# A two-layer block on one core: the broadcast inverse root mean squares written by ScalarE instead of copied by VectorE

## The reference, cut to what matters

```
proj = hidden_states @ W_in.T
u, gate = jnp.split(proj, 2, axis=-1)
... (causal convolution over 4 taps, silu)
ssm_p = u @ Wx.T
dt, Bm, Cm = jnp.split(ssm_p, [R, R + N], axis=-1)      # 32, 16 and 16 columns
dt = _rmsnorm(dt, dt_ln_w)      # x * rsqrt(mean(x * x) + 1e-6) * w
Bm = _rmsnorm(Bm, b_ln_w)
Cm = _rmsnorm(Cm, c_ln_w)
delta = jax.nn.softplus(dt @ Wdt.T + dt_bias)
# state = exp(delta * A) * state + delta * u * B;  y = sum(state * C), over 2048 tokens
```

## Time and profile before

| | |
|---|---|
| median of 3 runs | 2167.95 us (2166.07 to 2169.68) |
| the profiled execution | 2169.23 us |
| its span, first to last instruction | 2167.4 us |
| TensorE, granted clock | 0.804 of full |
| busy: TensorE / VectorE | 1693.6 us (78%) / 1427.1 us (66%) |
| busy: ScalarE / GpSimd | 1088.3 us (50%) / 1114.7 us (51%) |

### The profile page before, as it was taken

How to read it: one execution, slowest core, us unless ns; L and a number is a source line. 1 busy time by engine, 2 the same in 40 slices (tenths; PEclk the granted TensorE clock), 3 DMA queues, 4 the chain that set the end, 5 groups by cost and what they waited for, 6 DMA issues and landing times. The chain is left out here.

```text
span 2167.4 us, 24373 instructions
## 1 busy us (share of the span) xinstructions
PE 1693.6 (78%) x8224; PEld 899.0 (41%) x8224; DVE 1427.1 (66%) x2400; ACT 1088.3 (50%) x1988; POOL 1114.7 (51%) x617
## 2 busy tenths in 40 slices
PE   6865999999699947795786967969779687544678
PEld 2511222322274436563463635636447354222322
DVE  3263888884353120379888897887988889878131
ACT  2331666668321122557466574665646756543064
POOL 0000000000052032299999998999989899998102
PEclk9755999999857968795786978959779587556799
DMA  5332000000464454334434444444343444432301
GB/s 206 143 59 31 2 3 2 3 4 2 136 239 150 127 180 145 69 89 100 105 73 94 106 102 98 91 93 103 84 102 88 93 100 85 103 86 55 122 20 59
DMA packets 151262, 192.38 MB, mean 89 GB/s; under 512 B 18245, under 2 KB 123461, under 8 KB 149344
## 3 DMA queue, kind: packets, MB, share of 16 engines
q1 hardware_dynamic: 143250, 168.00, 31.1%
q0 software_dynamic: 4576, 16.79, 2.2%
q10 hardware_dynamic: 3312, 6.03, 0.7%
HBM read 142.60 MB, written 48.18 MB: 88 GB/s over the span
## 5 line engine op out<-in xcount | busy, mean ns | idle before, releaser
L1743 DVE TENSOR_TENSOR_SCAN ssm_scan<-ssm_psum,ssm_state,ssm_scan 128x256 f32<-128x256 f32 x1024 | 683.4, 729 | 53.2 <-ACT ssm_psum L1612 46.7
L1322 POOL TENSOR_TENSOR ssm_scan<-ssm_scan,ssm_bc 128x1024 f32<-128x1024 f32 x256 | 599.2, 2352 | 53.0 <-DVE ssm_state L1746 53.0
L1612 ACT ACTIVATE ssm_psum<-ssm_rep,ssm_a 128x256 f32<-128x256 f32 x1024 | 433.2, 467 | 258.0 <-DVE ssm_scan L1743 257.5
L1446 PE MATMUL ssm_psum<-ssm_scan,ssm_select 128*32 128x256 f32 x2048 | 213.2, 497 | 282.0 <-POOL ssm_scan L1322 281.7
L1307 POOL TENSOR_TENSOR ssm_scan<-ssm_rep,ssm_bc 128x1024 f32<-128x1024 f32 x160 | 376.5, 2354 | 58.9 <-PE ssm_psum L1446 48.4
L659 DVE TENSOR_REDUCE att_rowmax<-att_psum 128x1 f32<-128x512 f32 x448 | 278.1, 682 | 70.1 <-PE att_psum L554 70.0
L632 ACT ACTIVATE att_probs<-att_psum 128x1024 f32<-128x1024 f32 x256 | 248.5, 1021 | 147.6 <-PE att_psum L572 147.4
L1446 PEld LDWEIGHTS ssm_psum<-ssm_scan,ssm_select 128*32 128x32 f32 x2048 | 45.8, 122 | 404.3 <-POOL ssm_scan L1322 324.0
L532 POOL COPY att_v<-v_tokens 128x128 f32<-128x128 f32 x8 | 2.3, 291 | 360.3 <-ACT att_out L626 360.3
L554 PE MATMUL att_psum<-att_k,att_q 72*128 72x512 bf16 x448 | 160.5, 400 | 33.2 <-DMA att_k<-parts 32.1
L583 PE MATMUL att_psum<-att_probs,att_v 128*32 128x512 f32 x1024 | 139.0, 615 | 0.6 <-ACT att_probs L632 0.6
(11 more groups left out here) (231 smaller groups left out, 2073.8 us busy)
## 6 DMA issues: line engine op xcount, KB each, us to landing
ssm_rep<-drive_rows SPq DMA_DIRECT2D x256, 256.0 KB, 4.8
qkv_wmod<-in_wmod SPq DMA_DIRECT2D x8, 1536.0 KB, 12.1
moe_we<-in_we SPq DMA_DIRECT2D x8, 1024.0 KB, 14.4
ssm_bc<-bc_rows SPq DMA_DIRECT2D x32, 256.0 KB, 5.2
drive_rows<-ssm_delta SPq DMA_DIRECT2D x64, 128.0 KB, 1.7
drive_rows<-ssm_du SPq DMA_DIRECT2D x64, 128.0 KB, 1.8
sorted_rows<-moe_zeros SPq DMA_DIRECT2D x1, 5888.0 KB, 19.3
moe_sorted<-sorted_rows SPq DMA_DIRECT2D x23, 256.0 KB, 3.5
```

Source lines behind the costliest of these rows:

```text
L1322: nc.gpsimd.tensor_tensor(scan[:, Q % RING], scan[:, Q % RING], bc[:, c % 2, 1, gr, :].unsqueeze(1).to_broadcast([P, J, SW]), ALU.mult).th ...
L1446: last = nc.tensor.matmul(ps_y[t % 2][32 * j:32 * j + 32, :], select[:], scan[:, Q % RING, j, :], start=(gr == 0), stop=False)
L1612: nc.scalar.activation(ps_decay[n % HALF_BANKS][:, i], rep[:, s % 2, 0, j, :], ACT.Exp, scale=amat[:, t, gr, j:j + 1]).then_inc(decay_done, 1)
L1743: nc.vector.tensor_tensor_scan(scan[:, Q % RING, j, :], ps_decay[(2 * Q + j // 2) % HALF_BANKS][:, j % 2], scan[:, Q % RING, j, :], state[ ...
```

## The change

`inverse_rms` on ScalarE no longer writes the exponential into the small tile `rms`, from which VectorE copies. Its input, the logarithm in `rms`, is read broadcast, once for each of the three groups of columns, and the exponential goes straight into `rwide`. `rms_wide` and its two calls on VectorE go, and so does the semaphore `rms_done`; the wait for TensorE to have read the previous `rwide` (`rb_done`) moves to ScalarE. Also, the 16 semaphores of `attention` are now collected in `g.att_used`, and SP clears them at the start of `experts`, between its first load and its second.

```diff
--- before.py
+++ after.py
@@ -440,7 +440,7 @@
     STACK_LOADS = (2 * PAIRS + 1) * 16
     LOWEST = -3.4028234e38
     with ExitStack() as ctx:
-        sb, sem = sb_alloc(ctx, nc), sem_alloc(ctx, nc, "att")
+        sb, sem = sb_alloc(ctx, nc), sem_alloc(ctx, nc, "att", g.att_used)
         qst = sb("att_q", [P, (HEADS - 1) * T], BF16)
         kst = sb("att_k", [P, (HEADS - 1) * T], BF16)
         vcur = sb("att_v", [P, 2, KTILES, VC])
@@ -772,6 +772,8 @@
         @block.sync
         def _(sp):
             sp.dma_start(att[0:HEADS * E, :], scratch.num).then_inc(att_in, 16)
+            for semaphore in g.att_used:
+                sp.sem_clear(semaphore)
             sp.dma_start(rec[:], scratch.rec.unsqueeze(1).to_broadcast([HEADS, E, T])).then_inc(att_in, 16)
             sp.dma_start(wg[:], d["wg"].rearrange("(k p) m -> p k m", p=P)).then_inc(weights_in, 16)
             sp.dma_start(bg[:], d["bg"].to_broadcast([P, EXPERTS])).then_inc(weights_in, 16)
@@ -1141,12 +1143,12 @@
         scale, shift, gates = g.mod[:, 1, SCALE_A], g.mod[:, 1, SHIFT_A], g.mod[:, 1, GATE_A]
         (weights_in, win_in, diag_done, zeroed, x_in, mean_done, centred_done, square_done, var_done, logv_done, rstd_done, bcast_done,
          norm_done, h_done, halo_in, halo_saved, proj_done, upre_out, conv_done, conv_out, u_done, wx_done, proj_out, stat_done, rlog_done,
-         rms_done, rwide_done, rb_done, normed_done, bc_stored, b_set, wdt_done, abs_done, expneg_done, soft_done, relu_done,
+         rwide_done, rb_done, normed_done, bc_stored, b_set, wdt_done, abs_done, expneg_done, soft_done, relu_done,
          delta_done, du_done, drive_stored, decay_done, dve_input, pool_input, scan_done, carry_done, read_done, sum_done, summed,
          gate_mm, gate_out, gate_done, ygate_done, out_mm, x3_done, x3_stored, xres_in) = (sem(n) for n in (
              "weights_in win_in diag_done zeroed x_in mean_done centred_done square_done var_done logv_done rstd_done bcast_done "
              "norm_done h_done halo_in halo_saved proj_done upre_out conv_done conv_out u_done wx_done proj_out stat_done rlog_done "
-             "rms_done rwide_done rb_done normed_done bc_stored b_set wdt_done abs_done expneg_done soft_done relu_done "
+             "rwide_done rb_done normed_done bc_stored b_set wdt_done abs_done expneg_done soft_done relu_done "
              "delta_done du_done drive_stored decay_done dve_input pool_input scan_done carry_done read_done sum_done summed "
              "gate_mm gate_out gate_done ygate_done out_mm x3_done x3_stored xres_in").split())
         rep_in = [sem("rep_even_in"), sem("rep_odd_in")]
@@ -1188,7 +1190,7 @@
         SILU, ROWS_OUT, RMS, SQUARE, GATE_SILU, RSTD, H_OUT = 13, 16, 18, 19, 20, 21, 24
         STEP_OUT = {24: 0, 25: 1, 27: 2, 28: 3}
         CARRY_HALO, SAVE_HALO = {1: 0, 2: 1, 6: 2, 8: 3}, {4: 0, 5: 1, 8: 2, 10: 3}
-        CENTRED, RMS_WIDE, NORMED, NORM = 10, 18, 21, 22
+        CENTRED, NORMED, NORM = 10, 21, 22
         DELTA = {24: 0, 25: 1, 27: 2, 28: 3}
         RESIDUAL = {18: 0, 19: 1, 29: 2, 31: 3}
         GATE_Y, DRIVE = 2, 1
@@ -1558,7 +1560,10 @@
                     act.wait_ge(rwide_done, 3 * c)
                 nc.scalar.activation(flat, bank("square", c)[:, 0:3 * ST], ACT.Ln, bias=g.rms_eps[:, 0:1]).then_inc(rlog_done, 1)
                 act.wait_ge(rlog_done, c + 1)
-                nc.scalar.activation(flat, flat, ACT.Exp, scale=-0.5).then_inc(rms_done, 1)
+                if c >= 1:
+                    act.wait_ge(rb_done, c)
+                for s, (at, n) in enumerate(((0, RANK), (RANK, NST), (RANK + NST, NST))):
+                    nc.scalar.activation(rwide[:, :, at:at + n], rms[:, :, s:s + 1].to_broadcast([P, ST, n]), ACT.Exp, scale=-0.5).then_inc(rwide_done, 1)
 
             def step_out(c, pair):
 
@@ -1698,13 +1703,6 @@
                 nc.vector.tensor_reduce(halo[:, 2 * pair:2 * pair + 2, :], upre[:, pair % 2, :, SW:SW + TAPS - 1].unsqueeze(3), AX.X, ALU.max
                                         ).then_inc(halo_saved, 1)
 
-            def rms_wide(c):
-                dve.wait_ge(rms_done, c + 1)
-                if c >= 1:
-                    dve.wait_ge(rb_done, c)
-                for s, (at, n) in enumerate(((0, RANK), (RANK, NST), (RANK + NST, NST))):
-                    nc.vector.tensor_copy(rwide[:, :, at:at + n], rms[:, :, s:s + 1].to_broadcast([P, ST, n])).then_inc(rwide_done, 1)
-
             def rms_norm(c):
                 dve.wait_ge(rb_done, c + 1)
                 dve.wait_ge(stat_done, c + 1)
@@ -1769,7 +1767,6 @@
             for pair in range(DP):
                 carry_halo(0, pair)
                 save_halo(0, pair)
-            rms_wide(0)
             rms_norm(0)
             for pair in range(DP):
                 step_sizes(0, pair)
@@ -1785,8 +1782,6 @@
                             carry_halo(c + 1, CARRY_HALO[q])
                         if q in SAVE_HALO:
                             save_halo(c + 1, SAVE_HALO[q])
-                        if q == RMS_WIDE:
-                            rms_wide(c + 1)
                         if q == NORMED:
                             rms_norm(c + 1)
                         if q in DELTA:
@@ -1973,6 +1968,7 @@
         sb = sb_alloc(ctx, nc)
         g = Consts()
         g.used = []
+        g.att_used = []
         g.out_stored = [ctx.enter_context(nc.semaphore(f"out_{b}_stored")) for b in ("even", "odd")]
         g.ident = sb("ident", [P, P])
         g.inv_d = sb("inv_d", [P, P])
```

## The result

| | before | after |
|---|---|---|
| median of the runs, us | 2168.81 (6 runs, 2165.41 to 2174.84) | 2139.55 (6 runs, 2134.87 to 2145.55) |
| profiled execution: time / span, us | 2169.23 / 2167.4 | 2137.46 / 2135.6 |
| mean granted clock of TensorE | 0.804 | 0.809 |

The ratio is 0.9865, 95% interval 0.9842 to 0.9889: 29.3 us less.

The account below looks back on a forecast made before the run. GpSimd was taken to pace the state-space stage. From the profiled 2169.2 us, less 23.7 for the waits, plus 0.9 for the clears, came 2146.4; against the runs' median, 1.3 us lower, 2145.1 us, range 2137 to 2155.

Parts of the forecast that it names:

- The bound and the mechanism: State-space stage: GpSimd paces it; VectorE's three copies wait for the GpSimd instruction in progress, 5.79 us in chunk 1.
- The removal: Seven loop passes: GpSimd's waits for the carries of units 18 to 20 go with the copies, 23.7 us.
- What becomes late next: VectorE after the copies' place: new waits for two output products and the broadcast just fit; whole 23.7 us credited.
- The thin slack: GpSimd's new waits: 0.4 us or less in hand, so up to 0.5 us a chunk may return, 3.5 in all.
- ScalarE: Ahead of unit 18's decays: three exponentials replace one, 0.5 us more a chunk, covered by 2.5 us, cost nothing.
- Rival D: ScalarE in the loop: its writes wait for GpSimd's instructions, 3 x 2.35 = 7.1 us; slower, 2178 us; chance 0.02.
- rival F: Loop: copies' time is hidden anyway, ScalarE's added 0.5 us a chunk lands on the path; 2172.4 us; chance 0.01.
- The clears: Start of the experts' stage: 16 semaphore clears on SP delay the weight loads, +0.9 us, bounds 0 and 2.45.
- nothing hides it: Experts' stage: VectorE's first product waits for the last weight load, so the clears delay it by 0.9 us.
- B: Loop: output products at TensorE's lower clock delay VectorE, a new wait replaces half the old; 2157 us; chance 0.11.
- C: Loop: TensorE idles less and its clock holds longer, 8.6 us more gained; 2136.5 us; chance 0.08.
- E: Loop: delay passes to VectorE's next instruction, or ScalarE's three are as slow; no gain, 2168.9 us; chance 0.04.

Follow-up runs that it names:

- e1: Kernel before the change, with VectorE's three copies written as three tensor_reduce at the same place, no clears; ratio 0.9881, loop 1085.5 us.
- e3: Changed kernel with three copies of the old shapes back on VectorE at the old place, into an unused spare tile; ratio 1.0024, loop 1112.7 us.
- e7: Changed kernel with VectorE's third residual of the chunk before moved from place 29 to 30; ratio 0.9853, loop 1070.2 us.
- e8: As e7, with TensorE's third output product also moved from place 27 to 26; 2116.13 us, ratio 0.9756, loop 1055.5 us.
- e4: Changed kernel with one narrow copy (32 columns, into an unused spare tile) back on VectorE at place 18; ratio 0.9909, loop 1084.7 us.
- e5: Changed kernel with four more rounds of ScalarE's three exponentials, into a spare tile, right behind them; ratio 0.9896, loop 1082.0 us.
- a_again2: Changed kernel, unaltered, profiled once more; 2138.33 us, loop 1082.8 us.

## Why the prediction was right, point by point

**The bound and the mechanism.** Right, and shown: e1 takes the wait from the copies and nothing else, e3 puts such copies back and nothing else.

**The removal** was put at 23.7 us; the loop lost 23.4 in the profiled execution, and over all profiles it takes 1082.0 to 1085.5 us without the three copies and 1102.4 to 1112.7 with them (e7 and e8 apart). The gain is thus not one number: a chunk gives 1.58 or 3.76 us, by whether the third copy gets ahead of GpSimd's next product or waits for it.

**What becomes late next.** Right in each step of chunk 1: the wait for the output product (1.47 us), the carry of unit 20 with 0.4 us in hand, the broadcast just in time. The thin slack that made the range wide was enough, and e4 shows that it holds 1.2 us more of work at the place of the copies.

**ScalarE.** The three were put at 717 ns and took 490, since they overlap; either way they are hidden, and e5 shows cover for four times as many more. Rival D (ScalarE waits too) falls with the 213 ns, rival F (only what is added counts) with the 23.4 us of the loop and with e5.

**The clears.** This term was wrong, though it was small. Its size in the queue was right, 0.9 forecast and 0.95 measured. The step that failed is the next one, "nothing hides it": the experts' first product should have come 0.9 us later and did not. It came 12.35 us after the first load was issued before and 12.04 after. What held is the lower bound that the forecast named for this term, 0.

**What was missing.** The stretch from the experts' first product to the loop was taken to stay as it was, and in the profiled executions it was 6.1 us shorter. TensorE's clock has three courses there, and the two profiled executions took different ones. With this the profiled execution adds up: forecast 2146.4, measured 2137.46, 8.9 us apart, made up, within the rounding, of 6.1 for this stretch, 0.9 for the clears and 2.3 for the stretch ahead of the experts, less 0.3 in the loop. The median was 5.5 us below the forecast, so the range held, but how much of that is due to the clock's courses is not shown, since only profiled executions can be cut into stretches. The interval of the ratio, 24.1 to 34.3 us of 2168.8, allows the bare gain of the loop as well as some 10 us more.

**Rivals B and C.** B needed output products at the lower level ahead of unit 18; in chunk 1 they took 3.62 and 3.72 us, as before, and in each of chunks 2 to 6 the first again took 3.62 and the second 3.72. Its mechanism is real, though, at the end of the pass: a product of 5.02 us and 4.11 us of waiting. C had the clock give more, and the clock did, but in the experts' stage and not in the loop: GpSimd's waits for TensorE fell by 0.5 us only. (In e5 and a_again2 they fell by 2.7 and 2.4, the most that any kernel showed without a move in the tables.) E (the delay passes to the next instruction) is refuted by e1, where the instruction in the copies' place takes 176 ns.

## What to carry to other kernels

When an engine paces a stage, add up its waits and look at what stands ahead of each on the engine it waits for; a small instruction that lasts ten times longer than its size asks for is the one to replace, be it by another instruction on the same engine (the reduction of e1) or by another engine. Costs that depend on where two engines meet should be read in every pass and in more than one execution, and the slack behind them measured by spare work. After such a win, the same sum of waits shows the next one: two places in two tables, moved by one unit each, gave 29.8 us more (e8).

## What the runs showed of the hardware that I had not expected

- The same program can take one of several courses of TensorE's clock through a stage: the first 58, 66 or 70 us of the experts' stage, and no length between, with 1.00, 1.00 and 0.84 granted in the fourth to sixth window of the short one and 0.88, 0.50 and 0.50 in the middle one. What picks the course stays open.
- VectorE's copy of 32 columns waits for GpSimd whatever its tiles (e3, 2382 ns, other source and target), beside three copies in 0.37 us with GpSimd idle. GpSimd suffers little: its products took 2352 ns in the mean with the copies and 2357 without, and 2.38 us where a copy got ahead.
- Small activations in a row cost ScalarE less than their own durations: twelve in 1.63 us, 136 ns each, beside 213 to 256 ns for one.
